# A landmark-attention front split into two parts that run for two images side by side

## What is computed

```
x = x + gate(_gn(x))                        # L1: 1x1 convolution, times its input
t = t + landmark_attention(_ln_t(t))        # L2
t = t + top2_of_8_gelu_ffn(_ln_t(t))
...
kernel_1 = softmax(q @ k_lm.T * scale)      # 16 landmarks, 8 heads
kernel_2 = softmax(q_lm @ k_lm.T * scale)
kernel_3 = softmax(q_lm @ k.T * scale)
z = kernel_2.T / |kernel_2|^2
for _ in range(6):
    z = 2.0 * z - z @ kernel_2 @ z          # Newton
out = kernel_1 @ (z @ (kernel_3 @ v))
```

## Time and profile before

| | us |
|---|---|
| median of 3 runs | 5303.67 (5300.96 to 5309.0) |
| the profiled execution's own time | 5304.72 |
| its span | 5302.9 |
| PE busy | 4738.9 (89%) |
| DVE busy | 3577.1 (67%) |
| ACT busy | 2996.8 (57%) |
| POOL busy | 1023.8 (19%) |

### The profile page before, as it was taken

The page is one execution under the profiler, slowest core; times in us unless marked ns, Lnnn a source line. Parts: engine busy times, 40 slices in busy tenths (PEclk is TensorE's granted clock), DMA queues, the critical chain, the costliest instruction groups (busy, mean ns, idle before and its releaser), DMA issues.

```text
span 5302.9 us, 81731 instructions
## 1 busy us (share of the span) xinstructions
PE 4738.9 (89%) x25633; PEld 2629.4 (50%) x25633; DVE 3577.1 (67%) x7651; ACT 2996.8 (57%) x5516; POOL 1023.8 (19%) x1349
## 2 busy tenths in 40 slices
PE   6999999999999969588888888888999999999999
PEld 1222222222222223367777878777655555555554
DVE  6788888888888636556565655655577667667765
ACT  2666667676676724145555555557655554554552
POOL 2222223222232212023333333333100000000000
PEclk7999999999999989689999999999999999999999
DMA  2622223322233112235454554544211111111112
GB/s 61 166 78 69 73 66 98 84 66 77 66 92 83 49 31 28 68 111 169 135 169 138 154 152 145 162 132 134 64 49 52 45 48 51 47 47 51 49 45 76
DMA packets 396856, 461.35 MB, mean 87 GB/s; under 512 B 86136, under 2 KB 248144, under 8 KB 394320
## 3 DMA queue, kind: packets, MB, share of 16 engines
q1 hardware_dynamic: 362688, 409.11, 26.7%
q0 software_dynamic: 20576, 35.55, 2.4%
q10 hardware_dynamic: 13168, 11.48, 0.8%
HBM read 309.59 MB, written 129.84 MB: 83 GB/s over the span
## 4 chain that ended last, share of the span: by engine, by line
PE 34%; DVE 16%; issue 4%; DVEq 4%; ACT 2%; ACTq 0%; SPq 0%; DMA 0%
PE n_ps_f L2212 4%; PE n_ps_f L2205 4%; PE n_ps_xy L1860 4%; PE n_ps_h L1850 3%; PE n_ps_c L2252 3%; PE n_ps_h L2264 2%; PE n_ps_f L2199 2%; PE n_ps_f L1708 2%; DVEq L2084 1%; PE n_ps_xy L2268 1%; PE n_ps_f L1054 1%; DVE n_stats L1030 1%; PE n_ps_h L2268 1%; DVE n_xln L1042 1%; DVE n_down_weights L2083 1%
## 5 line engine op out<-in xcount | busy, mean ns | idle before, releaser
L664 ACT ACTIVATE a_probs<-ps_b 128x512 f32<-128x512 f32 x2048 | 1111.3, 595 | 558.7 <-PE ps_b L748 535.6
L496 DVE TENSOR_REDUCE a_negmax<-ps_a 128x1 f32<-128x1024 f32 x1024 | 1214.5, 1220 | 242.3 <-PE ps_a L696 213.0
L1663 ACT ACTIVATE n_hidden<-n_ps_h,n_b 128x128 f32<-128x128 f32 x1472 | 419.1, 373 | 346.9 <-PE n_ps_h L1850 346.1
L760 PE MATMUL ps_o<-a_probs,a_v_ones 128*32 128x512 f32 x4096 | 547.6, 607 | 0.5 <-ACT a_probs L664 0.5
L1860 PE MATMUL n_ps_xy<-n_down_weights,n_hidden 128*128 x2944 | 411.9, 284 | 79.2 <-ACT n_xy L1677 73.3
L696 PE MATMUL ps_a<-a_k_stack,a_q_stack 96*128 96x512 bf16 x1408 | 404.0, 394 | 58.5 <-DMA a_k_stack<-split_scratch 27.5
L748 PE MATMUL ps_b<-a_q_stack,a_k_stack 99*128 99x512 bf16 x1408 | 442.3, 386 | 14.8 <-ACT a_probs L664 11.9
L1860 PEld LDWEIGHTS n_ps_xy<-n_down_weights,n_hidden 128*128 128x128 f32 x2944 | 370.7, 196 | 117.3 <-issue 113.2
L2149 ACT ACTIVATE n_down_weights<-n_ps_h 128x512 f32<-128x512 f32 x288 | 172.2, 598 | 427.1 <-PE n_ps_h L2264 319.1
L1850 PE MATMUL n_ps_h<-n_xy,n_up_weights 128*128 128x128 f32 x2944 | 403.2, 281 | 3.2 <-issue 1.5
L1368 POOL DMA_INDIRECT rows_scratch<-n_xln,n_index_out x256 | 257.1, 1004 | 666.8 <-DVE n_index_out L1521 563.2
(11 more groups left out here) (349 smaller groups left out, 8154.3 us busy)
## 6 DMA issues: line engine op xcount, KB each, us to landing
n_up_weights<-in_L_ffn_W_dram SPq DMA_DIRECT2D x368, 256.0 KB
n_up_weights<-score_scratch SPq DMA_DIRECT2D x512, 128.0 KB, 2.9
split_scratch<-a_pieces SPq DMA_DIRECT2D x128, 256.0 KB
rows_scratch<-n_zero SPq DMA_DIRECT2D x16, 1472.0 KB, 9.6
outs_scratch<-n_xy SPq DMA_DIRECT2D x176, 128.0 KB
n_xg<-rows_scratch SPq DMA_DIRECT2D x80, 256.0 KB, 3.4
a_q_stack<-split_scratch SPq DMA_DIRECT2D x66, 256.0 KB, 5.0
a_k_stack<-split_scratch SPq DMA_DIRECT2D x66, 256.0 KB, 5.6
```

What stands on the lines that cost most here:

```text
L496: dve.tensor_reduce(negmax[:, b, t:t + 1], bank, axis=AX.X, op=ALU.max, negate=True).then_inc(ring_read, 1)
L664: act.activation(probs[:, m % PROBS, 512 * k:512 * k + 512], ps_b[:, k, :], ACT.Exp).then_inc(b_exp, 1)
L760: last = pe.matmul(ps_o[32 * j:32 * j + 32, 512 * k:512 * k + 512], v_ones[:, t, J * g + j, :], probs[:, (J * quad + j) % PROBS, 512 * k:5 ...
L1663: last = act.activation(hidden[:, j % 2, f, :], ps_h[j % 2][:, 128 * f:128 * f + 128], ACT.Gelu, bias=b1[:, bass.ds(e, 1), f:f + 1].rearra ...
```

## The change

The front is cut into a front, which ends with kernel_3 times v (kv) at slot 42, and a back: the Newton steps, the two small products behind them and the attention's output. Round i now runs front(i+3), back(i+2) and choice(i+1), in this order of the list; there are three passes ahead of the rounds instead of two, and round 13 has no front. The Newton half steps stand at consecutive slots from 1 to 13. What both parts use is doubled (`tok_next`, `m2t`, `kv`) and k1t has a tile of its own. PSUM's four banks are shared in another way: three rotate among the units of the front (`banks`, `bank_free`), the fourth (`pn`) belongs to the back. For that gate, tokens, q, k, v, s1, k1 and the copies go in halves of 512 columns, and so do the exponentials of k1 on ScalarE. `gate_choose_steps` takes the tiles in as many parts as its scratch has room for, with fewer slots in the landmark choice; the dense gate's scratch now lies in other tiles, in two halves of four tiles, and with that its sums over earlier tokens (L2063) move from slot 25 to slot 28 of the dense round.

In the diff `back` of VectorE comes first, then the exponentials of ScalarE, then `back` of TensorE.

```diff
+    for lo in range(0, NT, tiles):
+        shape = (128, tiles, E, E)
...
+        dve.tensor_tensor(above, other, own, ALU.is_gt)
+        yield dve.tensor_tensor(same, other, own, ALU.is_equal)
...
+        yield dve.tensor_reduce(rank[:, lo:lo + tiles, :], above, axis=AX.X, op=ALU.add)
...
+        banks, pn = (pa[:, 0:512], pa[:, 512:1024], pb_[:, 0:512]), pb_[:, 512:1024]
...
+        bank_of = {unit: banks[n % 3] for n, unit in enumerate(units)}
...
+                 wg=tok_nexts[0], wu=tok, above=tok_nexts[1][:, :, :], same=k1t[:, :], wd=tiled(xt2[:, :]), scores=up_weights, xt_other=part(0),
...
+            front, back = front
             side_by_side([front(0)])
-            side_by_side([front(1), choice(0)])
+            side_by_side([front(1), back(0)])
+            side_by_side([front(2), back(1), choice(0)])
...
-            experts(0, [front(2), choice(1)])
-            for i in range(1, B - 2):
-                experts(i, [front(i + 2), choice(i + 1)])
+            for i in range(B - 3):
+                experts(i, [front(i + 3), back(i + 2), choice(i + 1)])
+            experts(B - 3, [back(B - 1), choice(B - 2)])
...
+            def back(i):
+                yield 0
+                m2t, tok_next = m2ts[i % 2], tok_nexts[i % 2]
                 dve.tensor_scalar(z[:, :], m2t[:, :], fro[:, :], None, ALU.mult)
 
                 dve.tensor_scalar(zt[:, :], m2[:, :], fro[:, :], None, ALU.mult).then_inc(S["z0_up"], 1)
...
                 for it in range(NEWTON):
-                    yield 24 + 2 * it
+                    yield 1 + 2 * it
...
                     dve.wait_ge(mz_ps, i * NEWTON + it + 1)
-                    dve.tensor_copy(mz[:, :], pa[:, 0:128]).then_inc(mz_up, 1)
-                    yield 25 + 2 * it
+                    dve.tensor_copy(mz[:, :], pn[:, 0:128]).then_inc(mz_up, 1)
+                    yield 2 + 2 * it
                     dve.wait_ge(znew_ps, i * NEWTON + it + 1)
...
+                for k in range(HALVES):
+                    yield 35 + 2 * k
+                    tiles = slice(4 * k, 4 * k + 4)
+                    dve.wait_ge(S["attn_ps"], i * HALVES + k + 1)
+                    last = dve.tensor_tensor(tok[:, tiles, :], tok_next[:, tiles, :], pn[:, :].rearrange("p (t c) -> p t c", t=4), ALU.add)
+                    last.then_inc(S["attn_up" if k else "attn_half"], 1)
...
                 act.activation(e2[:, :], e2[:, :], ACT.Exp, scale=SCALE, accum_out=sum2[:, :]).then_inc(S["e_up"], 1)
...
-                act.activation(k1[:, :, :], k1[:, :, :], ACT.Exp, scale=SCALE).then_inc(S["e_up"], 1)
...
+                for k in range(HALVES):
+                    yield 22 + k
+                    act.wait_ge(S["d_up"], i * 3 + 2 + k)
+                    act.activation(k1[:, 4 * k:4 * k + 4, :], k1[:, 4 * k:4 * k + 4, :], ACT.Exp, scale=SCALE).then_inc(S["e_up"], 1)
...
+            def back(i):
+                m2t, kv = m2ts[i % 2], kvs[i % 2]
                 for it in range(NEWTON):
-                    yield 24 + 2 * it
+                    yield 1 + 2 * it
                     if it == 0:
                         pe.wait_ge(S["z0_up"], i + 1)
                     else:
                         pe.wait_ge(z_up, i * NEWTON + it)
-                    pe.matmul(pa[:, 0:128], m2t[:, :], z[:, :], start=True, stop=True).then_inc(mz_ps, 1)
-                    yield 25 + 2 * it
+                    pe.matmul(pn[:, 0:128], m2t[:, :], z[:, :], start=True, stop=True).then_inc(mz_ps, 1)
+                    yield 2 + 2 * it
                     pe.wait_ge(mz_up, i * NEWTON + it + 1)
...
+                    pe.matmul(pn[:, 128:256], zt[:, :], mz[:, :], start=True, stop=True)
+                    pe.matmul(pn[:, 256:384], mz[:, :], zt[:, :], start=True, stop=True).then_inc(znew_ps, 1)
```

More of the change, by code:

```diff
@@ L1743, in front @@
-                pe.wait_ge(S["m2_up"], i + 1)
-                pe.transpose(pa[:, 512:640], m2[:, :], ident).then_inc(S["norm_ps"], 1)
-                pe.wait_ge(S["fro_in"], i + 1)
-                pe.matmul(pa[:, 0:1], const["block16"], max2[:, :], start=True, stop=True).then_inc(S["norm_ps"], 1)
+                for k in range(HALVES):
+                    bank, half = begin("gate", k)
+                    pe.matmul(bank, w3[:, :], yt[:, half], start=True, stop=True).then_inc(S["front_ps"], 1)
@@ new lines, in front @@
+                yield 5
+                for k in range(HALVES):
+                    bank, half = begin("tok", k)
+                    pe.wait_ge(S["x2_up"], i * HALVES + k + 1)
+                    for t in range(4):
+                        col = 512 * k + 128 * t
+                        last = pe.transpose(bank[:, 128 * t:128 * t + 128], u[:, col:col + 128], ident)
+                    last.then_inc(S["front_ps"], 1)
+                yield 12
+                turned("lnt", xln)
+                for n, x in enumerate("qk"):
+                    yield 14 + n
+                    for k in range(HALVES):
+                        bank, half = begin(x, k)
+                        pe.wait_ge(*read(i, "lnt", k))
+                        pe.matmul(bank, wqkv[:, C * n:C * n + C], xt[:, half], start=True, stop=True).then_inc(S["front_ps"], 1)
@@ new lines, in front @@
+                yield 17
+                for k in range(HALVES):
+                    bank, half = begin("v", k)
+                    for t in range(4):
+                        col = 512 * k + 128 * t
+                        last = pe.matmul(bank[:, 128 * t:128 * t + 128], xt[:, col:col + 128], wqkv[:, 2 * C:3 * C], start=True, stop=True)
+                    last.then_inc(S["front_ps"], 1)
+                yield 19
+                bank, _ = begin("s2")
+                pe.wait_ge(S["lm_up"], i + 1)
@@ new lines, in front @@
+                pe.matmul(bank[:, 0:LM], q_lm[:, :], kt[:, 0:N:STEP], start=True, stop=True).then_inc(S["front_ps"], 1)
+                yield 20
+                for k in range(HALVES):
+                    bank, half = begin("s1", k)
+                    for t in range(4):
+                        col = 512 * k + 128 * t
+                        last = pe.matmul(bank[:, 128 * t:128 * t + 128], qt[:, col:col + 128], k_lm[:, :], start=True, stop=True)
+                    last.then_inc(S["front_ps"], 1)
@@ new lines, in front @@
+                yield 23
+                for k in range(HALVES):
+                    bank, half = begin("s3", k)
+                    pe.matmul(bank, q_lm[:, :], kt[:, half], start=True, stop=True).then_inc(S["front_ps"], 1)
+                yield 25
+                bank, _ = begin("norm")
+                pe.wait_ge(S["m2_up"], i + 1)
+                pe.transpose(bank[:, 128:256], m2[:, :], ident)
+                pe.wait_ge(S["fro_in"], i + 1)
+                pe.matmul(bank[:, 0:1], const["block16"], max2[:, :], start=True, stop=True).then_inc(S["front_ps"], 1)
@@ L1785, in front @@
-                last.then_inc(S["attn_ps"], 1)
+                pe.wait_ge(*read(i, "k1t", 1))
+                for k in range(HALVES):
+                    yield 34 + 2 * k
+                    if k:
+                        pe.wait_ge(S["attn_half"], i + 1)
+                    for t in range(4):
+                        col = 512 * k + 128 * t
+                        last = pe.matmul(pn[:, 128 * t:128 * t + 128], k1t[:, col:col + 128], mixed_p[:, :], start=True, stop=True)
+                    last.then_inc(S["attn_ps"], 1)
@@ L1928, in dense_attention_and_silu @@
     gate.update({n: sb("gate_" + n, [128, NT]) for n in ("top", "total", "picked")})
-    gate.update({n: sb("gate_" + n, [128, NT * E, E]) for n in ("above", "same")})
+    gate.update({n: shared[n].rearrange("p (a e) -> p a e", e=E) if n == "same" else shared[n].rearrange("p t (a e) -> p (t a) e", e=E) for n in ("above", "same")})
     chosen_before = by_expert(12, NT + 1)
```

312 lines of the change are left out of this document (160 added, 152 removed).

## The result

The changed kernel takes 5440.48 us (median of 4 runs, 5432.57 to 5441.7) against 5304.09 us (4 runs): a ratio of 1.0253, with a 95% interval of 1.0235 to 1.0271. It is slower by 2.5%, and 25 us above the 5415 of the forecast.

What follows compares the result with a forecast made beforehand. A round was taken as bounded by TensorE up to 10.9 us of waits. Rounds +77, passes and last round +20 and dense gate +13 summed to +110: 5415 us, forecast 5385 to 5445 (chance 0.52), range 5290 to 5490.

Steps and rivals of the forecast that it cites:

- The waits at slots 2 and 8: TensorE waits for the copy mz behind VectorE's choice norm and front norm, about 4 and 6 us in every round.
- Part A: Round's start, from VectorE's start of the next image's gate to TensorE's turning of the normed tokens: 23.7 to about 35.3 us.
- part B: The rest of a round, 67.2 us before: forecast to change by -5.65 us, to near 61.5.
- the first three terms: Lengthening VectorE's chain: scalings of z +0.5, first Newton step and second copy +2.7, tokens' copy behind a `hide` +0.9 us.
- The fourth: Fourth copy mz stands behind the front's norm, so TensorE's work comes after it; with six Newton products and a copy, +7.5 us.
- the slow stretch that I counted in part B: A third low-clock stretch of TensorE per round, following a wait, instead of two: +1.7 us, between -3.4 and +3.4.
- of the 2.25 us at 2687.10 ... -1.75: TensorE's wait ending a chain through the choice's exponential: 1.75 us of it leaves, as the norms lie further ahead.
- The table term: Two more ScalarE table loads of 1.28 us a round, half charged: +1.3 us, between 0 and 2.6.
- The passes: Three passes ahead of the rounds instead of two, at 49, 66 and 79 us: 194 against 151.8, +42.
- The dense gate: Its sums over earlier tokens move three slots, ahead of a tile's softmax: half of 1.93 us for 14 images, +13.
- The clock did not stay low in all of part A: Rival: two waits keep TensorE's clock low throughout the round's first part, +4.2 us a round, 5470 us; chance 0.13.
- VectorE did not get ahead: Rival: if kv comes soon, VectorE starts four us before TensorE and the slot 2 wait goes, 5245 us; chance 0.14.

Runs made afterwards that it cites:

- The two variants of the half steps: Changed kernel with Newton half steps moved behind the front's token norm: only the last six, to slots 14 to 19, 5351.92 us; all twelve, to slots 14 to 25, 5300.76 us.
- the read at slot 1: Changed kernel with VectorE's reading of kv moved from slot 42 to slot 1 of the next round: 5377.83 us, ratio 1.0148.

## Why the prediction was right

**The waits at slots 2 and 8** were forecast at some 4 and 6 us; they are 2.7 and 6.2 in the round above, 9.1 on average. The two variants of the half steps show that these waits, with the clock behind them, are what makes the kernel slower: without the second it gains 89 us, without both 140. That is the step on which the sign rested, and it held.

**Part A** was put at 35.3 us and is 37.8; **part B** at 61.6 and is 60.5. Of part A, the first three terms came out well: up to the front's norm it is 20.6 us (2724.41 to 2744.96) instead of 16.0, +4.6 against +4.1. The fourth is +9.5 against +7.5 (2744.96 to 2762.19, before 2675.12 to 2682.86), and the slow clock (2.1 us) is about the difference: the slow stretch that I counted in part B lies in part A, right behind the 6 us wait. TensorE's busy time grew by 1.8 us a round, near the 1.7 that I took for the clock, but in another shape, and that the two agree is in part luck: behind that wait the clock costs 2.1 us in the round above (9.64 at 0.78) and 4.6 in the round from 2624.84 (9.20 busy at 0.50), while part B of the round above ran at 0.94, much as before (0.95).

**What was mis-sized** is the gain in part B, "of the 2.25 us at 2687.10 ... -1.75". TensorE stands still in part B for 5.2 us (60.50 - 55.31), where the 7.4 of before and the forecast's terms (-2.1 -1.3 -1.75 -0.5 +0.5 +1.3) leave 3.5. Waits for ScalarE's moves did not fall: 4.8 us a round against 4.6. The wait ahead of the choice's exponential is gone, and one of 2.39 us stands at 2791.51, behind ScalarE's switches:

```profile
2781.50 1.28 ACT L1681 ACT_TABLE_LOAD   x1
2782.80 0.22 ACT L1681 ACTIVATE n_e<-n_e 128x16 f32<-128x16 f32 x1
...
2783.12 1.28 ACT L1721 ACT_TABLE_LOAD   x1
2784.42 1.14 ACT L1721 ACTIVATE n_hidden<-n_ps_h,n_b 128x128 f32<-128x128 f32 x4
2785.58 1.28 ACT L1685 ACT_TABLE_LOAD   x1
2786.87 1.15 ACT L1685 ACTIVATE n_xln<-n_xln 128x512 f32<-128x512 f32 x2
2788.04 1.28 ACT L1721 ACT_TABLE_LOAD   x1
...
2790.35 0.61 ACT L1735 ACTIVATE n_xy<-n_ps_xy 128x512 f32<-128x512 f32 x1
```

Besides, the copies in halves brought two short waits, for the turned tokens (L1806) and for those of kernel_3 (L1844), 1.3 us a round together, where I had only +0.5 for kv. I had -1.75 and +1.3 for the moves, and +0.2 came; with the 0.8 of the copies that makes some 1.5 of the 1.8 us by which a round is longer than forecast (99.0 against 97.2). The first full round, of 103.2 us (2422.18 to 2525.34), adds to it; why it is longer was not tried.

**The table term**, +1.3 between 0 and 2.6, was charged for a cost that neither run without the two loads gave back: in one the time stayed as it was, in the other it grew by 11 us. Both move the exponentials as well, so the loads' price in the changed kernel itself stays open. The next operation begins 0.02 us after the load here too (2781.50 + 1.28 to 2782.80), and the load at 2785.58 begins 0.02 us after the operation ahead of it (2784.42 + 1.14). So what the Trainium skill ("ScalarE: Activation LUTs", section "What ACT_TABLE_LOAD costs") adds for a drain does not show in this kernel. The larger sum that went with it, 5433, would have been near the result for the wrong reason.

**The passes** came out at +42.7 against +42, in part by luck: from one start of VectorE's transposes to the next they take 44.2, 62.6 and 82.7 us, put at 49, 66 and 79, and then 6.0 us pass until the first `up`, where it was 1.0 before. **The dense gate** is at +21.6 against +13: the place of the sums is worth 14.4, near the term; another 7 were not in it.

**The rivals.** The clock did not stay low in all of part A: 0.91 there. VectorE did not get ahead: it stood 6.44 us for kv. The first step of that rival was right and its condition was not met: once it is met, by the read at slot 1, the wait at slot 2 goes and the kernel gains 63 us. Its time was not right: with the wait at slot 8 in place the kernel is still slower than before.

## What to carry to other kernels

Before a short chain of steps is laid into a stretch of a round, look at what stands ahead of each of its instructions on the in-order engine: here a copy of 0.3 us sat behind a norm of 7.7 us, and the engine that carries all other work waited for it. A wait of TensorE costs more than its length where the clock falls behind it, so compare TensorE's busy time and its waits each for itself, before and after. A result that is only needed in the next round should not be read at the end of this one, ahead of the next round's start.

## What was not expected of the hardware

Of the 10.5 us by which a round shrank when the half steps moved, 4.4 came with TensorE's granted clock (0.99 instead of 0.92): as many instructions were busy 77.8 us instead of 82.2. Behind the 6 us wait it ran at 0.50, half of full speed and so 1.2 GHz, for 10 us in some rounds, and recovered sooner in others; rounds of some 98.3 and 99.6 us mostly alternate. The split did not bring the alternation: in the kernel before, rounds of some 93 to 95 us (clock 0.93 to 0.95) and of 88 to 90 us (0.98) mostly alternate too. And the variant that took 2.3 us of work from ScalarE has longer rounds, by some 5 us in every other one, in which a stretch of 12 us ran at 0.57 instead of 1.00.
